# Scattering the second graph's rows with GpSimd instead of permuting them with TensorE

## The reference

```python
# layer 0, per node: max over the first 25 neighbours' features (and 0), then a linear map
agg = feats.max(axis=2)
agg = jnp.where((degree <= S)[..., None], jnp.maximum(agg, 0.0), agg)
out = jax.nn.relu(jnp.einsum('bnf,fo->bno', concatenate([X, agg]), W) + b)
x = layernorm(x + out)
# layer 1: graph attention with 8 heads over the neighbours
Wh = (x @ W).reshape(Bx, Nx, H, HEAD_DIM)
e = leaky_relu(s1[:, :, None, :] + s2[:, None, :, :] + edge_emb[edge_types])
alpha = softmax(where(adj == 0, -1e9, e), axis=2)
h = einsum('bijh,bjhd->bihd', alpha, Wh)
x = layernorm(x + elu(layernorm(h) * gamma + beta))
```

## Time and profile before

| what | us |
|---|---|
| median of three runs | 3056.82 |
| lowest, highest | 3050.93, 3058.76 |
| the profiled execution | 3059.63 |
| its span on the core | 3057.9 |
| VectorE busy | 2525.2 (83%) |
| GpSimd busy | 2208.5 (72%) |
| TensorE busy | 2007.9 (66%) |
| ScalarE busy | 1058.5 (35%) |

### The profile page before, as it was taken

The page is one execution under the profiler, slowest core; times in us unless marked ns, Lnnn a source line. Parts: engine busy times, 40 slices in busy tenths (PEclk is TensorE's granted clock), DMA queues, the critical chain, the costliest instruction groups (busy, mean ns, idle before and its releaser), DMA issues.

```text
span 3057.9 us, 30468 instructions
## 1 busy us (share of the span) xinstructions
PE 2007.9 (66%) x6994; PEld 1423.7 (47%) x6995; DVE 2525.2 (83%) x5841; ACT 1058.5 (35%) x2587; POOL 2208.5 (72%) x2341
## 2 busy tenths in 40 slices
PE   8247566756666667766667667676677666477565
PEld 1134344534444445544455545554455444356453
DVE  6798887998888988889889988889896866577676
ACT  4223224333333333333443333333432222234334
POOL 3475567777777777777777777777777777777774
PEclk9968778777877788888888888887897887689787
DMA  8877667656666666766676666676655554445443
GB/s 300 258 229 227 205 213 220 187 171 191 203 184 207 189 195 209 216 208 188 205 218 193 195 205 217 190 220 193 198 156 143 158 147 132 128 134 170 128 134 91
DMA packets 282490, 577.75 MB, mean 189 GB/s; under 512 B 68801, under 2 KB 192706, under 8 KB 265922
## 3 DMA queue, kind: packets, MB, share of 16 engines
q0 software_dynamic: 109824, 305.79, 36.0%
q1 hardware_dynamic: 172482, 269.96, 26.4%
HBM read 488.78 MB, written 86.77 MB: 188 GB/s over the span
## 4 chain that ended last, share of the span: by engine, by line
POOL 43%; issue 18%; DVE 15%; PE 6%; DVEq 3%; DMA 3%; ACT 2%; POOLq 0%; ACTq 0%; SPq 0%
POOL ring L706 43%; DVE agg L1353 3%; DVEq L1126 3%; DVE pay L1172 2%; PE att_p L1016 2%; PE lin_p L979 1%; DMA ring<-nat_d,idx 1%; DVE ring L1492 1%; DVE agg L1344 1%; DVE pick L1230 1%; DVE adj_h L1159 1%; DMA ring<-table_d,top 1%; POOL pair_s L714 1%; PE score_p L952 0%; DVE lst L1251 0%
## 5 line engine op out<-in xcount | busy, mean ns | idle before, releaser
L706 POOL DMA_INDIRECT ring<-nat_d,idx x1096 | 1052.1, 960 | 390.6 <-issue 355.4
L706 POOL DMA_INDIRECT ring<-table_d,idx x1096 | 1046.2, 955 | 346.9 <-issue 332.0
L1016 PE MATMUL att_p<-ring,ident 128*128 128x256 f32 (+1 forms) x2384 | 575.2, 397 | 211.3 <-ACT x_t L809 125.6
L1016 PEld LDWEIGHTS att_p<-ring,ident 128*128 128x128 f32 (+1 forms) x2384 | 461.9, 198 | 327.4 <-issue 180.7
L1353 DVE TENSOR_REDUCE agg<-ring 128x256 f32<-128x2560 f32 (+9 forms) x120 | 473.1, 3942 | 2.7 <-issue 0.4
L979 PE MATMUL lin_p<-w_s,h_t 128*128 128x256 f32 x1024 | 428.9, 592 | 0.0
L979 PEld LDWEIGHTS lin_p<-w_s,h_t 128*128 128x128 f32 x1024 | 289.3, 296 | 123.1 <-issue 65.1
L837 ACT ACTIVATE neg<-z 128x256 f32<-128x256 f32 x128 | 53.3, 416 | 799.0 <-DVE z L1395 799.0
L1492 DVE TENSOR_TENSOR ring<-ring,score_p 128x1536 f32<-128x1536 f32 (+10 forms) x128 | 320.6, 2504 | 10.3 <-issue 1.0
L966 PE MATMUL turn_p<-ident,xs 128*128 128x128 f32 x256 | 65.5, 346 | 383.1 <-ACT h_t L802 365.0
L952 PE MATMUL score_p<-pay,pick 128*128 128x323 f32 x896 | 299.2, 482 | 18.9 <-DVE pick L1230 16.2
(11 more groups left out here) (193 smaller groups left out, 2868.8 us busy)
## 6 DMA issues: line engine op xcount, KB each, us to landing
adj_i<-in_adj_dram SPq DMA_DIRECT2D x128, 1024.0 KB, 5.7
sorted_d<-srt SPq DMA_DIRECT2D x112, 161.5 KB, 2.8
ring<-nat_d,idx POOLq DMA_INDIRECT x1096, 2.9
ring<-table_d,idx POOLq DMA_INDIRECT x1096, 2.9
table_d<-tab SPq DMA_DIRECT2D x128, 132.0 KB, 4.4
nat_d<-pay SPq DMA_DIRECT2D x32, 514.0 KB, 4.6
pay<-in_x_dram SPq DMA_DIRECT2D x32, 512.0 KB, 7.5
xs<-sorted_d SPq DMA_DIRECT2D x128, 128.0 KB, 4.1
```

What stands on the lines that cost most here:

```text
L706: pool.indirect_dma_start(out=to[:, k * width:(k + 1) * width], out_offset=None, in_=source, in_offset=bass.IndirectOffsetOnAxis(ap=idx_at ...
L1016: last = pe.matmul(att_p[:, 0:C], ident[0:on, :], r3[0:on, s, 0:C], start=(s == 0), stop=(s == k - 1))
```

## The change

Graph 1 (groups 4 to 7) is now sorted as graph 0 is. GpSimd issues the four scatters of a group right after the gathers of a tile: group 4 after tile 0, group 5 after tile 6, group 6 after tile 10, group 7 after tile 13 (SCATTERS). The 16 steps ("in", 16) to ("in", 31) go away on DVE, PE, ACT and SP. `pay_used` for groups 4 to 7 waits for `scattered` instead of `permuted`, and graph 1's lists are converted in rounds 10 and 12 instead of 12 and 14 (IDX_LEAD1). `own_first` holds two graphs, with one more small load.

```diff
+IDX_LEAD1 = (6, 4)
+DIRECT = 2
+SCATTERS = {0: 4, 6: 5, 10: 6, 13: 7}
...
+def idx_lead(b, part):
+    return (IDX_LEAD1 if b == 1 else IDX_LEAD)[part]
+
+
+def lists_in(r, part):
+
+    for b in range(1, B):
+        if r + idx_lead(b, part) == b * T:
+            return b
+    return None
...
-    for k in range(T, TILES):
+    for k in range(DIRECT * T, TILES):
         ins.setdefault(in_step(k), []).append(("in", k))
...
         def pay_used(eng, g):
-            if 0 <= g < GROUP:
+            if 0 <= g < DIRECT * GROUP:
                 eng.wait_ge(scattered[g % 2], 16 * GROUP * (g // 2 + 1))
-            elif g >= GROUP:
+            elif g >= DIRECT * GROUP:
                 eng.wait_ge(permuted, PERM_AT["in", GROUP * g + GROUP - 1] + 1)
...
             def load_idx(b, part):
                 for q in range(2):
-                    if b:
-                        sp.wait_ge(srt_out[q], 16 * (T // 2) * b)
+                    if b >= DIRECT:
+                        sp.wait_ge(srt_out[q], 16 * (T // 2) * (b - DIRECT + 1))
                     else:
-                        sp.wait_ge(scattered[q], 16 * GROUP * (GROUP // 2))
+                        sp.wait_ge(scattered[q], 16 * GROUP * (GROUP // 2) * (b + 1))
...
                 for part in range(2):
-                    b, u = (r + IDX_LEAD[part] + 1) // T, (r + IDX_LEAD[part] + 1) % T
-                    if u == 0 and 1 <= b < B:
+                    b = lists_in(r + 1, part)
+                    if b is not None:
                         load_idx(b, part)
+                        if b < DIRECT and part:
+                            load_own(b)
...
                     pool.indirect_dma_start(
-                        out=sorted_d[0], out_offset=bass.IndirectOffsetOnAxis(
+                        out=sorted_d[g // GROUP], out_offset=bass.IndirectOffsetOnAxis(
                             ap=rank_i[:, GROUP * g + t:GROUP * g + t + 1], axis=0),
...
                 if first(r):
                     gather(0, r)
+                if r in SCATTERS:
+                    scatter_rows(SCATTERS[r])
...
-                if g < GROUP:
-                    v.tensor_scalar(rank_i[:, GROUP * g:GROUP * (g + 1)], mine, float(GROUP), float(g),
+                if g < DIRECT * GROUP:
+                    v.tensor_scalar(rank_i[:, GROUP * g:GROUP * (g + 1)], mine, float(GROUP), float(g % GROUP),
                                     ALU.mult, ALU.add).then_inc(rank_put, 1)
```

More of the change, by code:

```diff
@@ L220, in build @@
         srt = [sb(f"srt{q}", [P, SENT]) for q in range(2)]
-        rank_i = sb("rank_i", [P, T], I32)
-        own_first = sb("own_first", [P, T * (SENT - OWN)])
+        rank_i = sb("rank_i", [P, DIRECT * T], I32)
+        own_first = sb("own_first", [P, DIRECT * T * (SENT - OWN)])
         own_in = sb("own_in", [P, TILES])
@@ L534, in load_idx, with load_own @@
                              .rearrange("(u p) k -> p u k", p=P)).then_inc(idx_ld, 16)
+            def load_own(b):
+                words = T * (SENT - OWN)
+                sp.dma_start(own_first[:, b * words:(b + 1) * words]
+                             .rearrange("p (g m c) -> p g m c", m=GROUP, c=SENT - OWN),
+                             sorted_d[b][:, OWN:SENT].rearrange("(m p g) c -> p g m c", p=P, g=GROUP))\
+                    .then_inc(own_ld, 16)
             def load_pay(g):
@@ L580, in _ @@
                     load_idx(0, 1)
-                    sp.dma_start(own_first[:, :].rearrange("p (g m c) -> p g m c", m=GROUP, c=SENT - OWN),
-                                 sorted_d[0][:, OWN:SENT].rearrange("(m p g) c -> p g m c", p=P, g=GROUP))                        .then_inc(own_ld, 16)
+                    load_own(0)
             load_adj(AHEAD + 3)
@@ L790, in copy_perm @@
                 if kind == "in":
-                    need(act, srt_out[k % 2], 16 * ((k - T) // 2))
+                    need(act, srt_out[k % 2], 16 * ((k - DIRECT * T) // 2))
                     act.activation(own_in[:, k:k + 1], perm_p[:, OWN:OWN + 1], ACT.Copy)
@@ L1222, in pick_rows @@
                     g, part = k // GROUP, k % GROUP
-                    if g < GROUP:
-                        dve.wait_ge(own_ld, 16)
+                    if g < DIRECT * GROUP:
+                        dve.wait_ge(own_ld, 16 * (g // GROUP + 1))
                         own = own_first[:, :].rearrange("p (k c) -> p k c", c=SENT - OWN)[:, :, 0]
@@ L1542, in _ @@
                 for part in range(2):
-                    b = (r + IDX_LEAD[part]) // T
-                    if (r + IDX_LEAD[part]) % T == 0 and 1 <= b < B:
+                    b = lists_in(r, part)
+                    if b is not None:
                         index_rows(b, part)
```

## The result

The changed kernel is slower. Its median is 3069.84 us (3064.12 to 3076.95, six runs), that of the kernel before 3056.26 us (3050.93 to 3058.76, six runs): ratio 1.0045, 95% interval 1.0035 to 1.0055. That is 13.6 us where 23.5 were predicted; the direction and the range (3066 to 3095) held, the size was 1.7 times too large.

The account below looks back on a forecast made before the run. GpSimd was taken to bound the kernel from its first layer 1 gather, VectorE before it. Three waits, net of removals, made VectorE 25.5 us late, less 2.0 in round 12: 23.5, so 3080 us, range 3066 to 3095.

Parts of the forecast that it names:

- What bounds the kernel: GpSimd works without real pause from its first layer 1 gather at 446.30 us; ahead of it VectorE is the bound.
- The added wait on ScalarE: Casts of tiles 28 and 32 wait for scatters to land, in rounds 3 and 7, making VectorE's `z` late.
- the second stall: Round 7: cast of tile 32 waits for group 6 until 276.6 us; `z` 23.4 us late, 2.7 more than the 20.7.
- VectorE's wait for the lists: Third wait, round 10: VectorE waits 7.7 us for graph 1's lists after group 7 lands, so it is 25.5 us late.
- I take 6 us: Estimated time for a graph 1 scatter to land, between the least (4.1 us) and the median (7.9) of the earlier trace.
- the list load: Load of graph 1's lists by SyncE after group 7's last scatter lands, taken as 6.9 us.
- the first stall: Round 3: cast of tile 28 waits for group 5 until about 229.7 us; `z` of round 4 25.4 us late.
- Its low end: Shift of about 13 us (3070) with scatters landing in 4.1 us and a list load of 3 us.
- Rival 1: Scatters come in time for ScalarE's cast at 201.3 us, only removals remain: 3038 us; chance 5%.
- Rival 2: No change: GpSimd's 34.8 idle us take the scatters and cover VectorE's stalls: 3057 us; chance 8%.
- Rival 3: Only the first of the three waits counts, with short landings: about 3070 us; chance 20%.
- Rival 4: Longer landings, or TensorE held at its lower clock by a longer pause, delaying `z`: 3088 to 3095 us; chance 17%.

Follow-up runs that it names:

- e3: Changed kernel with group 5 scattered one tile later, after tile 7 instead of tile 6: 3078.60 us, ratio 1.0071 to the kernel before.
- e11: Changed kernel, cast writing the degree to its own tile, groups 5, 6, 7 after tiles 5, 9, 12, lists in rounds 12 and 14: 3046.86 us.
- e10: Changed kernel, scatters unmoved, cast writing the degree to its own small tile, lists converted in rounds 12 and 14: 3051.29 us, ratio 0.9980.
- e4: Kernel before plus 16 same-size scatters into an unread DRAM tensor, after tiles 0, 6, 10 and 13: 3055.42 us, ratio 1.0002.
- e1: Changed kernel with groups 5, 6, 7 scattered earlier, after tiles 3, 6, 10: 3056.20 us, ratio 1.0000 to the kernel before.
- e2: Changed kernel with only group 5 scattered earlier, after tile 3 instead of tile 6: 3072.95 us, ratio 1.0054 to the kernel before.
- e9: Kernel before with only the cast writing the degree to its own small tile, nothing scattered for graph 1: 3059.60 us, ratio 1.0015.
- e8: Changed kernel, cast writing the degree to its own tile, groups 5, 6, 7 after tiles 4, 8, 11, lists in rounds 11 and 13: 3049.14 us.
- e5: Changed kernel with graph 1's lists converted in rounds 12 and 14 as before, scatters unmoved: 3065.61 us, ratio 1.0029 to the kernel before.

## Why the prediction was right on the side and too large

**What bounds the kernel: held.** In all twelve profiles the first layer 1 gather follows the store of the last table, and GpSimd keeps its pitch behind it. The words "never more than 3.9 us at once" were read from a single line of the view: the same view also has the 25.0 us of waits for VectorE named above, up to 6.7 us each, before and after alike, so the sum did not suffer. The end follows the yardstick: e3, 24.8 us more than before, is 22 us slower; e11, 8.7 us less, is 8 to 9 us faster. Median less yardstick lies between 2719.6 and 2726.8 us in all twelve.

**The added wait on ScalarE: held, mechanism and place.** Predicted: cast of tile 28 at 229.8 us, `z` at 238.4, cast of tile 32 at 276.6, `z` at 285.7, lists at 316.1. Measured: 223.5, 232.1, 267.3, 276.3, 302.1. Against the first layer 0 gather, `z` of round 4 was 22.2 us late (25.4 predicted), the reciprocal of round 7 17.2 us, that of round 9 17.3 us: the second stall, 9.1 us of idle time on ScalarE, made VectorE 0.1 us later and not 2.7. VectorE's wait for the lists was 3.1 us, not 7.7. e10 shows the cause by taking ScalarE's wait away with GpSimd's order unchanged: 14.3 us.

**The step that was mis-sized is the landing, "I take 6 us".** The last scatter of groups 5, 6 and 7 took 2.5, 2.5 and 4.0 us, and the list load 3.8 instead of 6.9. Put into the prediction's own steps this takes 3.5 us off the first stall; 2.9 off the second, and not another 3.5, because GpSimd's own pace now dates group 6; 2.0 off group 7; and 3.1 off the list load: 11.5 us. 23.5 less 11.5 is 12.0, and the yardstick shows 11.1. Part of the 14 us by which the lists came earlier than predicted is the 3.1 us by which this execution's gathers began earlier. The prediction named the reason for a short landing (no adjacency is loaded while casts stand still) and then took a value from a stretch in which it was loaded. The pause is not even needed. In e4, which is the kernel before with idle scatters added, three of them were issued from 216.6 to 219.2 us, between two adjacency loads, with a DMA share of 0.38 from 216 to 222 us:

```profile
DMA to landing us min/median/max: 2.5/2.6/2.6
```

What these short landings have in common is that no adjacency load ran beside them, whether ScalarE stood still or not. For the list load the prediction called the least value "not far below" 6.9 us; its own trace has 3.1 and 3.2 us for graph 0's two. Its low end, 13 us, used 4.1 us for the scatters and 3 us for the lists, and is near the truth.

**The estimate from the Trainium skill was put aside wrongly.** The Trainium skill, page "DMA: Bandwidth & Descriptors", section on the anatomy of a GpSimd DMA: 2.0 us plus the bytes over 436 GB/s, an estimated 2.4 us for one scatter. The prediction said that the trace disagrees, since the least landing was 4.1 us. That trace had no scatter in a quiet stretch. In the changed kernel's pause the landing is 2.5 us, and there the trace agrees with the page of the Trainium skill. In busier stretches it does not: 4.0 to 5.7 us for group 7, and in e1, where nothing pauses, 5.9 to 7.3 us for group 6.

**How the stalls add up: half right.** The sum went stall by stall, 25.4, then 2.7 more, then the lists, which suggests that the first is the largest. e2 shows that without it the time is the same: GpSimd's pace alone brings group 6 to 267 or 268 us. In the changed kernel too it was this pace, and not VectorE's round 6 as predicted, that dated group 6. The two dates lie close together, so the sum hardly suffered, but whoever mends the first stall alone wins nothing.

**The rivals.** Rival 1 (the scatters come in time, 3038) needed a date GpSimd did not make; and e1 shows that its price was wrong too: in time, the same kernel is at 3056. Its profile shows VectorE, quicker by the removals, waiting for rows behind the scatters, so GpSimd's 20 us of scatters then count. Rival 2 (no change) is refuted by the interval. Rival 3 (only the first stall, about 3070) gave the time and came near the mechanism: on VectorE the second stall added 0.1 us. But the second and third waits were there, and e2 shows that the first stall is not what the time hangs on. So the forecast of three stalls was right in direction and place, and it was partly luck that a mis-sized sum stayed in the range: the median, 3069.8, is that of rival 3 and of the low end. Rival 4 did not come: TensorE's granted clock was 0.54 of full, near its lower level of 1.2 GHz, in the pause, where it was busy 6.39 of 41 us, and 0.63 in the 39 us behind it, the 0.63 of the earlier trace rows.

**What stays open.** Why e10's median came out 6 us below its theory: 12.4 us are in the yardstick, and the rest is not assigned. Why the freed cast alone (e9) is 0.15% slower, though its way to layer 1 is no longer. And whether an order exists in which GpSimd's stretch up to tile 8 costs less than the 9 to 12 us of waiting still in e8 and e11.

## What to carry to other kernels

When a buffer is handed from one engine to another, ask which instruction of the waiting engine stands at the head of its queue and how early it stands: ScalarE's cast runs two rounds ahead of the search that really needs the half of `pay`, and all of ScalarE's round stood behind it. Giving that early instruction its own few words of memory, with the scatters where they were, turned a slowdown of 0.29% (e5) into a gain of 0.20% (e10). And before an early stall is blamed for a loss, work out the date at which the next one would fall without it.

## What the runs showed of the hardware

- A scatter of 128 rows of 1292 bytes took 2.5 us from issue to landing in the changed kernel's stage of a DMA share of 0.46 (182 to 223 us), and 5.9 to 6.6 us in that of 0.93 (112 to 150 us); before, it took up to 9.2 us. The share alone does not give the number, but four scatters in the changed kernel's pause and three in e4, where nothing paused, all of them without an adjacency load beside them, landed in 2.5 to 2.6 us. I had expected load to matter less.
- A gather takes GpSimd 1.25 us from one to the next and a scatter 1.27 us. In the kernel before, with VectorE busy for 29.75 of 32 us, GpSimd still issued 26 gathers in them.
- 16 scatters more in the kernel before, 2.6 MB, changed nothing that can be measured: 1.0002 (0.9993 to 1.0010).
